# VectorE adds the residual of every output row itself, GpSimd only sends; other output groups

## The reference

```python
x = x + layernorm(linear_attention(layernorm(x)))
x = x + layernorm(ffn(layernorm(x)))

def ffn(h):                                   # one expert of 16 for each row
    logits = h @ w_router.T
    top = one_hot(top_1(logits))
    scores = sigmoid(logits) * top
    inputs = scores.T[:, :, None] * h[None]   # only the chosen expert's row is not zero
    gate, up = split(inputs @ gate_up_proj)   # 16 experts, 128 -> 2 x 256
    expert_out = (up * silu(gate)) @ down_proj
    shared = silu(h @ w_gate.T) * (h @ w_up.T) @ w_down.T
    return shared + expert_out.sum(0)
```

## Time and profile before

| what | value |
|---|---|
| median of 3 runs | 321.18 us (319.95 to 321.85) |
| the profiled execution | 321.11 us, span 319.3 us |
| busy over the span: TensorE, VectorE, ScalarE, GpSimd | 85%, 86%, 60%, 60% |
| granted TensorE clock, mean | 0.954 of full speed |
| output sends (line 553) | 47, of 999 ns each |
| additions on GpSimd (line 545) | 34, 16.1 us together, 475 ns each |

### The profile page before, as it was taken

The page is one execution under the profiler, slowest core; times in us unless marked ns, Lnnn a source line. Parts: engine busy times, 40 slices in busy tenths (PEclk is TensorE's granted clock), DMA queues, the critical chain, the costliest instruction groups (busy, mean ns, idle before and its releaser), DMA issues.

```text
span 319.3 us, 6471 instructions
## 1 busy us (share of the span) xinstructions
PE 272.8 (85%) x1575; PEld 193.3 (61%) x1575; DVE 273.7 (86%) x1108; ACT 191.6 (60%) x583; POOL 190.4 (60%) x218
## 2 busy tenths in 40 slices
PE   6777999999999996897499899988599999999800
PEld 3443565556555652544366666677499999999700
DVE  7899999999999999996789999771059999999950
ACT  1744566566656652535358776335499999999400
POOL 5556577777777775300004556766004888888876
PEclk9999999999999999799579999999799999999975
DMA  7999910000000000000002111222796001111100
GB/s 242 391 413 413 418 45 0 4 1 0 2 0 2 2 0 0 0 3 1 0 0 70 67 68 69 85 85 100 234 359 210 28 25 38 40 44 36 35 20 0
DMA packets 12491, 28.34 MB, mean 89 GB/s; under 512 B 2049, under 2 KB 8076, under 8 KB 11944
## 3 DMA queue, kind: packets, MB, share of 16 engines
q1 hardware_dynamic: 9408, 21.57, 18.4%
q0 software_dynamic: 3040, 6.37, 5.9%
q10 hardware_dynamic: 8, 0.00, 0.0%
HBM read 15.31 MB, written 13.60 MB: 91 GB/s over the span
## 4 chain that ended last, share of the span: by engine, by line
DVE 41%; PE 35%; issue 9%; POOL 7%; ACT 4%; DMA 2%; DVEq 0%; ACTq 0%; POOLq 0%; SPq 0%
PE banks L1230 13%; PE banks L1249 6%; DVE hT_e L1164 5%; POOL sorted_rows L535 5%; DVE rows L1171 3%; DVE rows L1135 3%; POOL out L553 2%; PE banks L1266 2%; DVE stats L1186 2%; DVE num L913 2%; PE banks L1410 2%; PE banks L1218 2%; PE banks L1350 2%; ACT ya L635 1%; DVE stats L1029 1%
## 5 line engine op out<-in xcount | busy, mean ns | idle before, releaser
L508 POOL TENSOR_TENSOR kv<-qk,vv 128x1024 f32<-128x1024 f32 x32 | 62.4, 1951 | 2.5
L1230 PE MATMUL banks<-kv,upto 128*128 128x512 f32 x128 | 60.7, 597 | 1.0 <-POOL kv L508 1.0
L553 POOL DMA_INDIRECT out<-rows,token_i x47 | 47.0, 999 | 10.5 <-issue 5.8
L1410 PE MATMUL banks<-xsT,w_now 128*128 128x128 f32 x376 | 52.2, 284 | 0.2 <-DVE hT_e L1164 0.2
L535 POOL DMA_INDIRECT sorted_rows<-rows,slot_i x32 | 31.7, 992 | 28.9 <-DVE slot_i L977 19.2
L1410 PEld LDWEIGHTS banks<-xsT,w_now 128*128 128x128 f32 x376 | 47.0, 197 | 1.0 <-issue 0.9
L502 POOL TENSOR_TENSOR qk<-ex,rl 128x256 f32<-128x256 f32 x32 | 23.3, 728 | 36.9 <-ACT ex L608 36.9
L889 DVE TENSOR_TENSOR prod<-banks,qk 128x1024 f32<-128x1024 f32 x32 | 38.9, 1215 | 0.6 <-PE banks L1230 0.2
L913 DVE TENSOR_REDUCE num<-prod 128x128 f32<-128x1024 f32 x32 | 38.6, 1208 | 0.0
L1164 DVE TENSOR_TENSOR hT_e<-silu_e,banks 128x256 f32<-128x256 f32 x47 | 19.3, 411 | 16.6 <-ACT silu_e L753 14.7
L1249 PE MATMUL banks<-w_qkvo,xnT 128*128 128x384 f32 x64 | 28.1, 523 | 6.1 <-DVE zq L875 3.9
(11 more groups left out here) (202 smaller groups left out, 663.6 us busy)
## 6 DMA issues: line engine op xcount, KB each, us to landing
sorted_rows<-rows SPq DMA_DIRECT2D x7, 780.0 KB, 13.8
rows<-sorted_rows SPq DMA_DIRECT2D x10, 520.0 KB, 6.6
w_exp<-in_gate_up SPq DMA_DIRECT2D x4, 1024.0 KB, 20.5
w_exp_out<-in_down SPq DMA_DIRECT2D x4, 512.0 KB, 21.5
x_then_down<-in_x SPq DMA_DIRECT2D x2, 768.0 KB, 7.7
out<-rows,token_i POOLq DMA_INDIRECT x47
sorted_rows<-rows SPq DMA_DIRECT2D x1, 650.0 KB, 19.5
x_then_down<-in_x SPq DMA_DIRECT2D x2, 256.0 KB, 3.6
```

What stands on the lines that cost most here:

```text
L508: nc.gpsimd.tensor_tensor(kv[:, u, :].rearrange("p (h m d) -> p h m d", h=NH, m=HD), k, v, ALU.mult).then_inc(s_kv, 1)
L553: nc.gpsimd.indirect_dma_start(out=out_rows, out_offset=bass.IndirectOffsetOnAxis(ap=token_i[:, j - 1:j], axis=0), in_=rows[:, j - 1, 0:D] ...
L1230: ins = nc.tensor.matmul(ps_s[u % 2][:, cols], upto[:], kv[:, u, cols], start=True, stop=True)
L1410: ins = nc.tensor.matmul(ps_gue[u % 2][:, c * P:(c + 1) * P], w_now[:, u % 2, c * P:(c + 1) * P], xsT[:, u % 2, :], start=True, stop=True)
```

## The change

VectorE uses the fused instruction (multiply by the factor, add the residual) for all 47 tiles. GpSimd's loop is left with the sends. The groups are ten of four tiles, then one of 3, one of 2 and one of 2; before they were 2, 2, 2, 3, 3, eight of 4 and a last one of 3. The extra series steps, which before went to the early groups (`many`, `most`), now go to the steps after tile 42 (`last`), and in those steps two rows may be scaled.

```diff
-        ENDS = [2, 4, 6, 9, 12] + list(range(16, ST, 4)) + [ST]
+        ENDS = list(range(4, ST - 4, 4)) + [ST - 4, ST - 2, ST]
         GROUPS = list(zip([0] + ENDS, ENDS))
...
-        ADDED_BY_POOL = 34
...
-            for j in range(ST + 1):
-                if j < ADDED_BY_POOL:
-                    x1 = flat(rows[:, j:j + 1, 0:D])
-                    pool.wait_ge(s_yn, j + 1)
-                    nc.gpsimd.tensor_tensor(x1, x1, flat(rows[:, j:j + 1, D:2 * D]), ALU.add).then_inc(s_fin, 1)
-                if j > 0:
-                    if j <= ADDED_BY_POOL:
-                        pool.wait_ge(s_fin, j)
-                    else:
-                        pool.wait_ge(s_fin_last, j - ADDED_BY_POOL)
...
+            for j in range(ST):
+                pool.wait_ge(s_fin, j + 1)
+                if j in (0, TOKENS_FIRST):
+                    pool.wait_ge(s_token, 1 + (j > 0))
+                nc.gpsimd.indirect_dma_start(
+                    out=out_rows, out_offset=bass.IndirectOffsetOnAxis(ap=token_i[:, j:j + 1], axis=0),
+                    in_=rows[:, j, 0:D], in_offset=None,
+                    bounds_check=NTOK - 1, oob_is_err=False).then_inc(s_out, 16)
...
-                if i < ADDED_BY_POOL:
-                    nc.vector.tensor_scalar(r, r, rstd3[:, i:i + 1], None, ALU.mult).then_inc(s_yn, 1)
-                else:
-                    nc.vector.scalar_tensor_tensor(out=x1, in0=r, scalar=rstd3[:, i:i + 1], in1=x1,
-                                                   op0=ALU.mult, op1=ALU.add).then_inc(s_fin_last, 1)
+                nc.vector.scalar_tensor_tensor(out=x1, in0=r, scalar=rstd3[:, i:i + 1], in1=x1,
+                                               op0=ALU.mult, op1=ALU.add).then_inc(s_fin, 1)
...
+            def scale_if_ready():
+                nonlocal scaled
+                if scaled < ST and begun > GROUP_OF[scaled] + (left > 0):
+                    scale_row(scaled)
+                    scaled += 1
...
-                many, most = begun in (1, 2, 3), begun == 1
+                last = begun > len(GROUPS) - 3
...
-                chain_steps(1 + many)
+                chain_steps(1 + last)
...
-                chain_steps(1 + most)
-                if scaled < ST and begun > GROUP_OF[scaled] + (left > 0):
-                    scale_row(scaled)
-                    scaled += 1
-                if scaled == 1:
-                    scale_row(scaled)
-                    scaled += 1
-                chain_steps(1 + many)
+                chain_steps(1 + last)
+                scale_if_ready()
+                if last:
+                    scale_if_ready()
+                chain_steps(1 + last)
...
-                chain_steps(1 + most)
+                chain_steps(1 + last)
```

More of the change, by code:

```diff
@@ L413, in build @@
         s_series3 = sem("norm_steps3")
-        s_yn = sem("ffn_scaled")
         s_token = sem("tokens_ready")
         s_fin = sem("output_ready")
-        s_fin_last = sem("last_outputs_ready")
         s_out = sem("output_stored")
@@ L1192, in _ @@
             while scaled < ST:
-                if begun > GROUP_OF[scaled] + (left > 0):
-                    scale_row(scaled)
-                    scaled += 1
+                scale_if_ready()
                 chain_steps(2)
```

## The result

The changed kernel took 315.94 us, the median of four runs from 315.17 to 316.95; before it was 321.19. The ratio is 0.984, with a 95% interval of 0.980 to 0.988: faster by 1.6%, against a forecast of 315.3 us. On another chip, C, the same two kernels stood the other way round, 337.3 against 324.4. Both are this document's subject: first what the change does where nothing disturbs it, then what chip C showed. Times given are medians of all runs, while ratios compare only runs within 1.5% of their kernel's fastest (fast ones), so that on chips A and C a time can lie further off than its ratio says.

What follows compares the result with a forecast made beforehand. GpSimd was taken as the bound since 263 us, at 1.662 us a tile. With 1.475 us a step, row 37 sent at 299.4 and nine more starts at 1.288, 321.11 - 5.83 gives 315.3 us; range 313.4 to 318.0.

Steps and rivals of the forecast that it cites:

- (1): GpSimd loses 34 additions, 0.374 us each where it is full: 8.2 us after 263.06, more than can be won.
- (2): VectorE's row instruction becomes the fused one, 288 to 346 ns median: a price of 0.06 us a tile.
- (3): VectorE's loop, no longer held up by additions (stalls about 0.29 us a tile), goes from 1.518 to 1.475 us a step.
- rival B: Loop: no stall left, TensorE's pace of 1.455 us a step, end at 311.1, 314.4 us in all; chance 0.15.
- stalls by sends: VectorE's loop: a send holds a series step 0.26 us in three steps of four, 1.29 + 0.75 x 0.26 = 1.49 us.
- (4): Start of the loop: groups of four bring the first send some 2.5 us later, near 244, at no cost.
- The sum: End of kernel: row 37 sent at 299.4, nine more starts at 1.288 us, end 312.0 against 317.83: 5.83 us less.
- VectorE's own end: Tail: last row ready at about 307.9, GpSimd reaches row 45 at 309.7, so small last groups hide by 1.8 us.
- A: Loop gets no faster, sends hit VectorE as often as before: 1.518 us a step, 317.0 us; chance 0.22.
- C: GpSimd stays the bound, sends slowed by VectorE's fused instruction to 1.57 us each: 321 us as before; chance 0.06.
- D: VectorE's fused instruction is caught in every send: 1.70 us a step, 3.4 us slower, 324.5 us; chance 0.05.
- series steps of 0.3 to 0.4 us: Sign in VectorE's changed profile: series steps this long should still stand in the middle of sends.

Runs made afterwards that it cites:

- kernels with spare additions: Changed kernel plus unneeded GpSimd additions for tiles 0 to 33: each before its own tile's send, 344.2 us; before the previous tile's send, 327.5 us.
- plain tail: Changed kernel with groups of four to the end, a last one of 3, no doubled series steps or second rows: 333.5 us on chip A, 314.8 on B.
- three kernels of chip A: Kernel before with fused instruction alone, 334.4 us; changed kernel without doubled last steps and small last groups, 333.5; changed kernel with doubled steps seven tiles earlier, 335.5.
- additions in turn: Changed kernel plus unneeded GpSimd additions for tiles 0 to 33, addition of tile j before send of tile j - 1: 327.5 us against 324.4, ratio 1.011.

## Why the prediction was right, and where not

**What bounds the kernel** was read rightly: GpSimd, 1.66 us a tile. The two kernels with spare additions show it from the other side, since they give VectorE the fused instruction and yet do not gain: one ends where GpSimd's 2.29 us a pair put it (344 us), the other, with 1.66 us a pair, takes 327.5 us beside 324.4, and the 3 us between them are one stall at the end of the loop.

**(1) The additions.** As forecast, more went than could be won; GpSimd now waits for VectorE before most sends, up to 0.5 us beyond the 0.30 that always lie there.

**(2) and (3) The step.** From tile 4 at 238.88 to tile 46 at 300.95 it is 42 steps of 1.478 us, forecast 1.475. That this mean agrees is luck. Up to tile 45, at 298.61, the step is 59.73 / 41 = 1.457 us, which is the pace of TensorE and of rival B, and no mean of stalled and free steps. The last step alone takes 2.34 us: it is full of VectorE's doubled series steps and second row, and in the kernel with the plain tail it takes 1.34. One step more is long, 1.82 us from 253.41 to 255.23, where VectorE's `token_i` lies.

So the stalls by sends that the prediction reckoned with (0.75 x 0.26 us a step) were not there. I had read the series step at 295.68 as held by a send. With sends alone no instruction with two SBUF inputs is held up to speak of: 149 ns for line 143, 344 ns for the fused instruction. That makes the 0.06 us of part (2) no price either, since the multiplication had a mean of 366 ns beside additions and sends. Only line 137 is held, the integer `TENSOR_SCALAR` with one input, in the last part of a send (323 ns against 164 without sends). The rule that the prediction weighed and put aside, of the Trainium skill, page "SBUF — State Buffer", section "Who interferes with whom", says just that of two SBUF inputs: they contend with GpSimd's reads and not with its writes. The trace agrees. What I took for the send was, as it seems, the rest of the addition ahead of it: where a send had to wait for its own addition, it waited 0.8 us beyond the addition's recorded end and started 1.28 us after the addition's start. Before the send at 295.29 GpSimd has:

```profile
294.63 0.49 POOL L545 TENSOR_TENSOR rows<-rows 128x128 f32<-128x128 f32 x1
```

An estimate from these rows fits: 294.63 + 1.28 us, and 0.16 us for the series step itself, is 296.07, and the step ended at 296.10. The Trainium skill, page "Perfetto Trace Analysis", section "GPSIMD Engine Instruction", warns that GpSimd's recorded spans are unreliable and that start-to-start spacing is to be used; the 0.8 us agree.

**(4) The groups.** The first send is at 246.70, 14.1 us after tile 0; the forecast's 244 was 12.9 after it. It cost nothing, as forecast. The new groups alone gained nothing (323.23 against 322.49 us), and the small last groups nothing either (314.8 without them, 315.2 with).

**The sum.** Row 37 was forecast at 299.4 with tile 4 at 237.10, so 62.3 behind it; measured, 300.83 - 238.88 = 61.95. The end was forecast 74.9 behind tile 4 and is 312.65 + 0.98 - 238.88 = 74.75. VectorE's own end lies 2.6 us under the sends, forecast 1.8. The path is right, and the sum holds in part because errors cancel: tile 45 comes some 0.75 us sooner behind tile 4 than reckoned, row 37's send comes 2.2 us behind it and not 1.8, and the last ten sends take 0.2 us more. The forecast lies 1.6 us under the profiled execution; that is the later start of the loop (tile 4 1.8 us later than before), less the 0.15.

**The rivals.** A, C and D did not come: the step is shorter, and the sends take 0.98 us as before, but for a few of up to 1.10. Of B the mechanism came, no stall and TensorE's pace, but not its end: it puts that 74.0 us behind tile 4, 0.75 too early, mostly by the time to row 37's send and the spacing of the last ones, which all of the prediction's cases share. But on chip C, and by the three kernels of chip A very likely there too, the change is a loss of 4%, and the prediction has no case for it. Its slower rival was about VectorE's port, not about TensorE's semaphores; its 0.05 was a chance for a mechanism that no run showed. What the profile of before could have said is little: its trace has no late update. hT_e of tile 46, forecast at 298 to 300, is at 300.95 by the later start, and series steps of 0.3 to 0.4 us, forecast beside sends, are there for line 137 alone.

**What stays open.** Why TensorE's updates are late on two chips and not elsewhere, whether that and the missing updates are one thing, and whether they would be late without the recording of the profile, under which all these runs were made. The density of the sends matters: at 1.66 us spacing none showed in the loop, at 1.3 to 1.5 they did. But spacing alone, without additions, was not tried, nor another way to send, nor was the kernel before profiled on chip A or C.

## What to carry to other kernels

When the chain that ended last finishes in a queue of one engine, look on that engine's own timeline how far back it has been full: here it had been for 54 us, and not for the 10 that the chain showed. Then ask for the next bound before adding up what is removed; 12.7 us of GpSimd's work went, and 5.3 us came back. Look at a mean in parts before calling it right: here 41 steps at one pace and one of 2.34 us made the forecast mean by luck. And measure a change that brings transfers closer together on more than one chip: the kernel that was nearly 2% faster in two comparisons was 4% slower in the third.

## What the runs showed of the hardware that was not expected

- Releases by TensorE can come late: in the changed kernel on chip C up to 2.5 us after the matmul's modelled end, in the kernel with additions in turn once 4.4 and then 5.7 us; on chips A and C only, and beside output sends of GpSimd that start 1.3 to 1.5 us apart. Of VectorE and ScalarE none that the trace has was late in the changed kernel.
- On chips A and C the trace lacks many updates of semaphores once the output sends begin: it has 389 of 752 of the sends' own for the changed kernel on chip C and 218 for the new groups alone on chip A, against at least 719 on chip B.
- The same program on different chips: 315.2 and 337.3 us, and 314.8 and 333.5 for the plain tail. The kernel before differs far less, 321.2 to 324.4.
- An indirect send of 128 rows of 512 bytes starts every 1.29 us at best (0.98 and 0.30). An addition of 128x128 on GpSimd is recorded with 0.48 us, but a send that waits for it starts 1.28 us after its start; with the wait moved behind the next addition the pair takes 1.66 instead of 2.29 us.
- Each send's completion is 16 updates of its semaphore. The Trainium skill, page "DMA: Bandwidth & Descriptors", section "Why a DMA increments its semaphore by 16 and not by 1", says that each of 16 DMA engines posts one; the trace agrees: on chip B the posts of a send end within 0.3 us of each other in 41 of the 47 sends, and up to 1.5 us apart in the others.
